# Mixtures of experts: own row buffers, tile-by-tile choice and tile tables split between two engines

## The reference

```python
# mixture 0: E, K, I = 32, 4, 128, no capacity
logits = x @ gate_w.T + gate_b
topk_logits, topk_idx = jax.lax.top_k(logits, K)
topk_weight = jax.nn.softmax(topk_logits, axis=-1)
# tokens are sorted by expert; for each: gate and up (with biases), clip, activation, down (with bias)
y = jnp.sum(outs * topk_weight[..., None], axis=1)

# mixture 1: 128 old experts of which 48 are kept, TOP_K = 8, CAP = 96
logits = x @ gate_weight.T
logits = jnp.where(old_to_new[None, :] == -1, -jnp.inf, logits)
top_v, top_i = jax.lax.top_k(softmax(logits), TOP_K)
top_v = top_v / jnp.sum(top_v, axis=-1, keepdims=True)
pos = jnp.sum(jnp.cumsum(oh, axis=0) * oh, axis=-1) - 1      # place within the expert
valid = pos < CAP
```

## Time and profile before

| | |
|---|---|
| median of three runs | 4206.21 us |
| the profiled execution's own time | 4202.31 us |
| its span | 4200.6 us |
| TensorE, matmuls, busy | 3276.3 us (78%) |
| VectorE busy | 2831.2 us (67%) |
| ScalarE busy | 2240.0 us (53%) |
| GpSimd busy | 1801.6 us (43%) |
| mean granted TensorE clock | 0.868 |

### The profile page before, as it was taken

The page is one execution under the profiler, slowest core; times in us unless marked ns, Lnnn a source line. Parts: engine busy times, 40 slices in busy tenths (PEclk is TensorE's granted clock), DMA queues, the critical chain, the costliest instruction groups (busy, mean ns, idle before and its releaser), DMA issues. The chain is left out here.

```text
span 4200.6 us, 68597 instructions
## 1 busy us (share of the span) xinstructions
PE 3276.3 (78%) x19706; PEld 2591.1 (62%) x19707; DVE 2831.2 (67%) x6281; ACT 2240.0 (53%) x5922; POOL 1801.6 (43%) x3107
## 2 busy tenths in 40 slices
PE   7799947916888379079999999999647399999274
PEld 3355545715776267058778878788545288888253
DVE  5699946746777566378768778588363388888542
ACT  3699802405777134068768678588212266665021
POOL 0399913567663145636446356356138200000265
PEclk9799967968999589589999999999757699999566
DMA  2011132430000335310000000000324300000524
GB/s 83 24 48 48 43 141 78 138 103 15 1 1 1 141 95 137 98 50 19 18 11 19 14 14 19 11 18 19 129 64 67 101 1 1 1 1 1 178 50 103
DMA packets 133310, 221.36 MB, mean 53 GB/s; under 512 B 28912, under 2 KB 106608, under 8 KB 131264
## 3 DMA queue, kind: packets, MB, share of 16 engines
q1 hardware_dynamic: 99216, 147.84, 10.6%
q0 software_dynamic: 33792, 69.83, 7.5%
HBM read 162.60 MB, written 54.80 MB: 52 GB/s over the span
## 5 line engine op out<-in xcount | busy, mean ns | idle before, releaser
L1256 POOL DMA_INDIRECT ex_xr<-scratch_rows,mo_token x288 | 286.6, 995 | 347.5 <-issue 312.0
L598 POOL TENSOR_TENSOR sc_h<-sc_h,sc_c 128x512 f32<-128x512 f32 x256 | 326.9, 1290 | 193.4 <-DVE sc_h L635 185.3
L3029 DVE TENSOR_TENSOR sa_pT<-bank,sa_pT 128x512 fp32r<-128x512 f32 x512 | 329.9, 686 | 34.2 <-ACT sa_pT L2897 30.3
L2889 ACT ACTIVATE sa_p<-bank,sa_nm 128x512 f32<-128x512 f32 x512 | 346.7, 689 | 2.5 <-DVE sa_nm L3020 2.5
L635 DVE TENSOR_TENSOR_SCAN sc_h<-sc_da,bank 128x512 f32<-128x512 f32 x256 | 311.1, 1220 | 37.9 <-ACT sc_da L578 22.9
L2718 PE MATMUL bank<-sa_kT,sa_qT 128*128 128x512 f32 x1024 | 333.4, 437 | 1.5 <-DVE residual L2996 1.5
L3016 DVE TENSOR_REDUCE sa_mx<-bank 128x2 f32<-128x1024 f32 x256 | 312.2, 1220 | 26.4 <-PE bank L2720 22.0
L1370 ACT ACTIVATE ex_xT<-bank 128x256 f32<-128x256 f32 (+1 forms) x288 | 105.1, 365 | 416.6 <-PE bank L1304 395.5
L2742 PE MATMUL bank<-sa_pT,sa_v 128*128 128x256 f32 x2048 | 301.4, 290 | 16.9 <-DVE sa_pT L3029 16.3
L1322 PE MATMUL bank<-mo_w_gu,ex_xT 128*128 (+2 forms) x1152 | 311.9, 399 | 1.3 <-issue 0.7
L2742 PEld LDWEIGHTS bank<-sa_pT,sa_v 128*128 128x128 f32 x2048 | 260.4, 190 | 39.3 <-DVE sa_pT L3029 28.7
(11 more groups left out here) (401 smaller groups left out, 9417.2 us busy)
## 6 DMA issues: line engine op xcount, KB each, us to landing
scratch_ys<-ex_yo SPq DMA_DIRECT2D x192, 128.0 KB
mo_w_gu<-in_w_gu SPq DMA_DIRECT2D x2, 9216.0 KB, 27.3
sc_c<-scratch_c SPq DMA_DIRECT2D x64, 256.0 KB, 3.2
sa_share<-scratch_shares SPq DMA_DIRECT2D x256, 64.0 KB, 2.6
mo_w_dn<-in_w_dn SPq DMA_DIRECT2D x2, 4608.0 KB, 48.0
mo_w_dn<-in_w_dn SPq DMA_DIRECT2D x2, 4096.0 KB, 33.3
scratch_rows<-ln_stage POOLq DMA_DIRECT2D x64, 128.0 KB, 5.5
ex_xr<-scratch_rows,mo_token POOLq DMA_INDIRECT x288
```

The costliest lines, as they stand in the source:

```text
L598: pool.tensor_tensor(h, h, C[u], ALU.mult).then_inc(used.sem, 1)
L1256: pool.indirect_dma_start(xr[u][:, :], None, rows, bass.IndirectOffsetOnAxis(ap=token[:, i:i + 1], axis=0), bounds_check=rows.shape[0] - 1 ...
L2889: act.activation(pr[h][:, :], SC[2 * s_ + h][:, :], ACT.Exp, bias=nm[:, col:col + 1], scale=SCALE, accum_out=rs[:, col:col + 1]).then_inc( ...
L3029: dve.tensor_tensor(spot(1), PT[h][:, :].rearrange("p (k n) -> p k n", k=TPB), spot(0).bitcast(F32), ALU.subtract).then_inc(*inc("kept_d"))
```

## The change

Four things are changed, all in `layer_norm` and `moe`.

- The ring of normalised rows has 16 buffers instead of four when rows are stored, so that VectorE's waits for it fall away; the stores still count in four semaphores.
- The logits of a tile go to one of four banks, and each tile is counted; TensorE waits before its fifth tile's logits, and every later one's, until VectorE has added the bias to the tile four before. VectorE adds the bias, takes the maxima and finds the indices tile by tile in the same block, the maxima one tile behind the add, the indices two behind. In mixture 0 it splits the experts' biases ahead of the first of these.
- In mixture 0 ScalarE clears the two bias tables, ahead of its exponential, instead of GpSimd.
- In mixture 0 VectorE compares all of a chunk's tile numbers in one operation into a new table `tile_is`, and ScalarE scales it, one tile of tokens at a time, into `tile_hot`. TensorE waits for both.

Cut to its core:

```diff
@@ layer_norm @@
-        RING = 4 if rows is not None else 2
+        RING = TILES if rows is not None else 2
...
                         pool.dma_start(rows[0][i * P:(i + 1) * P, 0:D_MODEL], normal(i)) \
-                            .then_inc(rows[1][i % RING].sem, 16)
+                            .then_inc(rows[1][i % 4].sem, 16)
...
                     if i >= RING:
                         dve.wait_ge(turned.sem, turned.at(i - RING + 1))
-                        if rows is not None:
-                            dve.wait_ge(rows[1][i % RING].sem, rows[1][i % RING].at(16 * (i // RING)))
@@ moe, logits @@
-                LG = c.banks[2:2 + EB]
+                LG = c.banks[2:6]
...
+                    if i >= 4:
+                        pe.wait_ge(ldone.sem, ldone.at(i - 3))
                     for k in range(KC):
-                        last = pe.matmul(LG[i // TPBANK][:, (i % TPBANK) * E:(i % TPBANK + 1) * E],
+                        last = pe.matmul(LG[i % 4][:, 0:E],
...
-                    if i == TILES - 1:
-                        last.then_inc(logit.sem, 1)
+                    last.then_inc(logit.sem, 1)
 
                 def add_bias(dve):
                     if which == 0:
                         dve.wait_ge(loaded.sem, loaded.at(16 * len(LOADS)))
-                    dve.wait_ge(logit.sem, logit.at(1))
-                    for g in range(EB):
...
+                        sp_ = Steps(dve, bsplit)
+                        sp_.then(dve.tensor_copy(bparts[0][:, :], braw[:, :]))
+                        sp_.then(dve.tensor_tensor(braw[:, :], braw[:, :], bparts[0][:, :], ALU.subtract))
+                        sp_.then(dve.tensor_copy(bparts[1][:, :], braw[:, :]))
+                        sp_.then(dve.tensor_tensor(braw[:, :], braw[:, :], bparts[1][:, :], ALU.subtract))
+                        sp_.then(dve.tensor_copy(bparts[2][:, :], braw[:, :]))
+
+                    for i in range(TILES + 2):
+                        if i < TILES:
+                            dve.wait_ge(logit.sem, logit.at(i + 1))
+                            dve.tensor_tensor(lg[:, i * E:(i + 1) * E], LG[i % 4][:, 0:E], bias[:, :], ALU.add) \
+                               .then_inc(ldone.sem, 1)
+                        if 1 <= i <= TILES:
+                            j = i - 1
+                            dve.wait_ge(ldone.sem, ldone.at(j + 1))
+                            dve.max(top[:, j * 8:(j + 1) * 8], lg[:, j * E:(j + 1) * E]).then_inc(own.sem, 1)
+                        if i >= 2:
+                            j = i - 2
+                            dve.wait_ge(own.sem, own.at(max(2 * j, 1)))
+                            dve.max_index(topi[:, j * 8:(j + 1) * 8], top[:, j * 8:(j + 1) * 8],
+                                          lg[:, j * E:(j + 1) * E]).then_inc(own.sem, 1)
@@ moe, GpSimd @@
-                        for b in (b_gu, b_dn):
-                            pool.memset(b[:, :].bitcast(F32), 0.0).then_inc(blanked.sem, 1)
@@ moe, TensorE @@
                         pe.wait_ge(slotted.sem, slotted.at(ch + 1))
-                        if cap is not None:
-                            pe.wait_ge(hid_made.sem, hid_made.at((ch + 1) * TPC))
+                        pe.wait_ge(hid_made.sem, hid_made.at((ch + 1) * TPC))
@@ moe, ScalarE @@
+                    if cap is None:
+                        for b in (b_gu, b_dn):
+                            dst = b[:, :].bitcast(F32).rearrange("p (r n) -> p r n", n=D_MODEL)
+                            act.activation(dst, c.zeros[:, :].bitcast(F32).rearrange("p (r n) -> p r n", r=1)
+                                           .to_broadcast([P, dst.shape[1], D_MODEL]), ACT.Copy).then_inc(blanked.sem, 1)
                     act.wait_ge(expd.sem, expd.at(1))
                     act.activation(wk, wk, ACT.Exp).then_inc(expd.sem, 1)
+                    if cap is None:
+                        act.wait_ge(made.sem, made.at(5))
+                        for i in range(TILES):
+                            ch, u = divmod(i, TPC)
+                            if u == 0:
+                                act.wait_ge(slotted.sem, slotted.at(ch + 1))
+                                if ch >= 2:
+                                    act.wait_ge(marked.sem, marked.at(ch - 1))
+                            cut = slice(u * K * NT, (u + 1) * K * NT)
+                            act.activation(tile_hot[ch % 2][:, cut], tile_is[ch % 2][:, cut], ACT.Copy,
+                                           scale=id1[:, i:i + 1]).then_inc(hid_made.sem, 1)
@@ moe, VectorE @@
-                    for i in range(TILES):
-                        dve.max(top[:, i * 8:(i + 1) * 8], lg[:, i * E:(i + 1) * E]).then_inc(own.sem, 1)
-                    dve.wait_ge(own.sem, own.at(TILES))
-                    for i in range(TILES):
-                        dve.max_index(topi[:, i * 8:(i + 1) * 8], top[:, i * 8:(i + 1) * 8],
-                                      lg[:, i * E:(i + 1) * E]).then_inc(own.sem, 1)
...
                         for ch in range(CHUNKS):
                             rows_of(ch, rowf)
-                            for n in range(PER):
-                                e = ch * PER + n
-                                last = dve.tensor_scalar(tile_hot[ch % 2][:, n * NT:(n + 1) * NT], iota_e[:, 0:NT],
-                                                         tilef[:, e:e + 1], id1[:, e // K:e // K + 1],
-                                                         ALU.is_equal, ALU.mult)
-                            last.then_inc(slotted.sem, 1)
+                            if ch >= 2:
+                                dve.wait_ge(hid_made.sem, hid_made.at((ch - 1) * TPC))
+                            dve.tensor_tensor(
+                                tile_is[ch % 2][:, :].rearrange("p (n r) -> p n r", r=NT),
...
+                                .to_broadcast([P, PER, NT]), ALU.is_equal).then_inc(slotted.sem, 1)
...
-                    if which == 0:
-
-                        sp_ = Steps(dve, bsplit)
...
```

More of the change, by code:

```diff
@@ L783, in moe @@
             iota_e = sq("mo_iota_e", [P, max(NT, P)])
+            top, topi = sq("mo_top", [P, TILES * 8]), sq("mo_topi", [P, TILES * 8], U32)
+            if which == 0:
+                bparts = [sq(f"mo_bpart{i}", [E, GU + D_MODEL], BF16) for i in range(3)]
             with ExitStack() as qq:
                 xnT = qq.enter_context(nc.sbuf_tensor("mo_xnT", [P, KC * TOKENS], F32, allow_name_mangling=True))
-                LG = c.banks[2:2 + EB]
+                LG = c.banks[2:6]
                 def logits(pe, i):
@@ L812, in moe @@
                            last_step=add_bias, rows=(rows, rowed), late_loads=late_loads)
-            logit.counted(1)
-            ldone.counted(EB)
+            logit.counted(TILES)
+            ldone.counted(TILES)
             upper = sq("mo_upper", [P, P], BF16)
-            top, topi = sq("mo_top", [P, TILES * 8]), sq("mo_topi", [P, TILES * 8], U32)
             hot = sq("mo_hot", [P, TK * E])
@@ L835, in moe @@
                 texp = sq("mo_texp", [NT, 1])
-                bparts = [sq(f"mo_bpart{i}", [E, GU + D_MODEL], BF16) for i in range(3)]
                 rowi, tilei = sq("mo_rowi", [P, TK], I32), sq("mo_tilei", [P, TK], I32)
                 rowf, tilef = sq("mo_rowf", [P, TK]), sq("mo_tilef", [P, TK])
+                tile_is = [sq(f"mo_tile_is{u}", [P, PER * NT]) for u in range(2)]
                 tile_hot = [sq(f"mo_tile_hot{u}", [P, PER * NT], F32R) for u in range(2)]
@@ L1031, in _ @@
                             rows_of(ch, rowf)
-                            for n in range(PER):
-                                e = ch * PER + n
-                                last = dve.tensor_scalar(tile_hot[ch % 2][:, n * NT:(n + 1) * NT], iota_e[:, 0:NT],
-                                                         tilef[:, e:e + 1], id1[:, e // K:e // K + 1],
-                                                         ALU.is_equal, ALU.mult)
-                            last.then_inc(slotted.sem, 1)
+                            if ch >= 2:
+                                dve.wait_ge(hid_made.sem, hid_made.at((ch - 1) * TPC))
+                            dve.tensor_tensor(
+                                tile_is[ch % 2][:, :].rearrange("p (n r) -> p n r", r=NT),
+                                iota_e[:, 0:NT].rearrange("p (o r) -> p o r", o=1).to_broadcast([P, PER, NT]),
+                                tilef[:, ch * PER:(ch + 1) * PER].rearrange("p (n o) -> p n o", o=1)
+                                .to_broadcast([P, PER, NT]), ALU.is_equal).then_inc(slotted.sem, 1)
                     else:
@@ L1063, in moe @@
                          (expd, 2), (ranked, 1), (counted_, 1), (weighted, 1),
-                         (hid_made, 0 if cap is None else TILES),
+                         (hid_made, TILES),
                          (tagged, 0 if cap is None else 16), (blanked, 2 if cap is None else 0),
```

## The result

The changed kernel takes 4140.7 us (median of 4 runs) beside 4206.1 for the kernel before in the same job: ratio 0.984, 95% interval 0.982 to 0.986. It is 65 us faster, where 127 were forecast, and lies outside the range of 4052 to 4100.

What follows compares the result with a forecast made beforehand. It took the serial chain from layer norm to first gather in each of four mixtures as the bound; savings of 30.9 twice, 31.5 and 33.6, together 126.9, off the 4206.2 median gave 4079 us, range 4052 to 4100.

Steps and rivals of the forecast that it cites:

- Row buffers: Layer norm and logits: with 16 slots no store is waited for; saves 16.2 per mixture 0, 28.5 and 30.6 in mixtures 1.
- Split forward: Mixture 0's logits: VectorE's bias split before the first bias add makes TensorE wait 1.9 us at the fifth tile.
- Choosing in the logits: Logits: tile-by-tile choosing hides under TensorE's 1.17 us a tile; next block starts 2.8 us after the last copy.
- Clears on ScalarE: Mixture 0, block after the logits: clears take 7.2 us, Exp ends at 8.8, next step comes sooner; 5.2 us saved.
- Mixture 1, 3.0 us each: Block after mixture 1's logits: index cast starts earlier but is held to the end of GpSimd's small operations; 3.0 saved each.
- Tables: Mixture 0's tables: one compare replaces eight operations, two chunks take 5.3 us, eight chunks 23.2 for 26.5; 3.3 us saved.
- the bound of 6.3 for a ScalarE free of charge: Mixture 0's tables: upper bound on the saving, 6.3 us, if ScalarE's scaling cost nothing.
- Bias DMAs: Mixture 0, token to first gather: six bias DMAs issue and land while VectorE works; 1.3 for 9.4 us, 8.1 saved.
- TensorE's clock: Rival, logits: unbroken work raises the clock to the 2.4 GHz level, 26 us more gained, 4053 us; 12 in 100.
- The weights as a bound: Rival, before the first expert: row stores delay the weights' landing until TensorE waits, kernel slower, 4215 us; 2 in 100.

Runs made afterwards that it cites:

- the weights held: Changed kernel with SyncE's transfers of the weights and the sum held until all sixteen row stores have landed: 4073.5 us, ratio 0.968.
- the kernel without the first part of the change: Changed kernel with four row buffers and experts chosen after the logits as before; split forward, ScalarE's clears and scaling, one-piece tables kept: 4175.7 us, ratio 0.992.
- the last experiment: Kernel before, four row buffers kept, with SyncE's transfers of the weights and the sum held until all sixteen row stores have landed: 4122.6 us, ratio 0.980.

## Why the prediction was wrong

1. **Row buffers, 91.5 us: the step that failed.** "Their landing is needed only by the gathers and the tag store, over 20 us later." It is needed by the block's end too, through GpSimd's DRAIN. The copies themselves came as said: fourth at 572.75, sixteenth at 588.76, 16.0 later. But the landing didn't move with the rows. Issued all at once behind the weights, the stores landed at 598 and 3027.8. From the first row to the next block the changed kernel saved 26.4 us over the four mixtures, and VectorE alone stood idle for 62.3 at the blocks' ends. The old ring had hidden this: it let GpSimd issue its last store only when most had landed, and the DRAIN was 2.7 us. The wait on the store didn't go, it moved from the ring to the block's end. The three runs with the weights held, the buffers alone and the rows on SyncE show it from three sides.
2. **Split forward, 1.9 us:** TensorE waited 1.59 before the fifth tile's logits (576.65), in mixture 0 only. GpSimd's stores didn't hold the casts.
3. **Choosing in the logits:** hidden under 1.17 us a tile. The 2.8 us to the next block held where the stores had landed (2.7 with the weights held).
4. **Clears on ScalarE:** next block to count copy 9.40 us, forecast 9.6, with the Exp ending 8.7 behind the block's start and VectorE waiting 3.79 for it.
5. **Mixture 1, 3.0 us each: too little.** The cast wasn't held to the end of GpSimd's small operations: it ran at the block's start, in 0.29 us. Next block to count copy saved 4.5 and 4.7. The Trainium skill, "SBUF — State Buffer", section "Who interferes with whom", has the shared port held for one instruction at a time, and this cast agrees with it; I had let the row of the memsets speak against it. Why the cast of mixture 0 was held through both memsets no run here shows. The trace shows the reverse as well: GpSimd's select, which ran beside VectorE's comparison of two inputs, took 1.76 and 5.85 us and ended 0.2 us behind that comparison each time. In the kernel without the first part of the change, where VectorE was still looking for maxima and indices, it took 0.29.
6. **Tables:** 625.83 to 649.28 is 23.4 us, forecast 23.2; the round for two chunks is 5.34 (636.59 to 641.93), forecast 5.3. Three buffers, which end it, gave 4.1 us a mixture. With the 3.1 that the change itself gave (26.5 less 23.4) that is over 7 us, more than the bound of 6.3 for a ScalarE free of charge: the prediction's own 2.1, 1.94 and 0.15 put that bound at 7.6 (the last chunk starts at 7 x 2.1 = 14.7 and ends 4.2 later, for 26.5), which would have taken the range 2.6 us further down.
7. **Bias DMAs:** the gather comes 1.27 us behind the token, forecast 1.3.

Of the rivals, a block's end that waits for the stores was not among them. TensorE's clock did not rise in the logits, through 19 us of nearly unbroken work; the row of busy times for that stretch of the changed kernel (length, PE, PEld, DVE, ACT, POOL, granted clock, DMA share, GB/s):

```profile
571.30:590.30 19.00, 17.38 (x88) 16.87 (x86) 10.96 (x68) 5.38 (x14) 7.76 (x13) 0.50 0.98 420
```

The weights as a bound didn't come either. Held back until 577.74 and beyond, they landed at most 46.7 us after their issue, ahead of the gather in all four mixtures. The warning that I passed over is a DMA share of 0.85 in the logits of a mixture 1, and 0.98 in the row above. I had reasoned that a late landing harms nobody before the gather, and never listed who waits for a store's landing at the block's end. The row of L174 for GpSimd's queue before, 2.7 us where SyncE's is 0.12, was there to be read.

## What to carry to other kernels

When a buffer wait is removed, ask what else waits for the same transfer: the landing stays where the DMA engines put it, and the next thing that needs it, here the end of the block through GpSimd's DRAIN, inherits the wait. Read the DRAIN rows of each queue, before as well. And look at who fills the DMA engines first: transfers that are needed tens of us later should not be issued ahead of small ones that gate the chain.

## What the runs showed of the hardware

GpSimd's DRAIN lasted until its own stores had landed (2.7 us before, 5.2 to 6.9 with the weights held, 23.1 to 36.8 in the changed kernel), SyncE's did not (0.12 us, with over 20 us of weights to come in the changed kernel and its own stores under way in the run where it stores the rows). SyncE's queue took stores slowly behind the weights, one issue lasting 14.27 us for 0.33 at least, and that held the block's end as well, by 3.3 and 4.0 us. A store of 128 KB landed 2.0 us after its issue at the least, 19 to 20 behind the weights of mixture 0 and 33.4 to 33.5 behind those of mixture 1 (the last four of each). And stages that no edit touched moved by some us from kernel to kernel: the first row was stored between 564.2 and 569.1, and between the chains the changed kernel lost 7.0 us to the one before, the one with the weights held 2.6 and the last experiment 10.5. What moves them stays open.
